# Layer kernel on one core: the second norm's scaling moved behind the feed-forward layers, a weight load issued later, and high-part passes ordered ahead of the low part

## The reference

```
h = layernorm(x, ln1_s, ln1_b)
q, k, v = h @ Wq + bq, h @ Wk + bk, h @ Wv + bv
x = x + (linear_attention(q, k, v) @ Wo + bo)
h = layernorm(x, ln2_s, ln2_b)
x = x + (relu(h @ W1 + b1) @ W2 + b2)
```

## Time and profile before

| what | us |
|---|---|
| median of 3 runs | 608.91 |
| lowest and highest of them | 607.68, 609.31 |
| the profiled execution, its own time | 609.01 |
| its span, first to last instruction | 607.1 |
| what lies around the span | 1.9 |

### The profile page before, as it was taken

One profiled execution on the slowest core, in us unless ns is written; L12 is line 12 of the kernel. 1 busy time (PEld: TensorE's weight loads), 2 busy tenths in 40 slices (PEclk: granted clock), 3 DMA queues, 4 the chain that ended last, 5 costly groups with the idle time before them and its releaser, 6 DMA issues.

```text
span 607.1 us, 13106 instructions
## 1 busy us (share of the span) xinstructions
PE 574.8 (95%) x4578; PEld 539.1 (89%) x4578; DVE 438.4 (72%) x1412; ACT 394.8 (65%) x1392; POOL 269.3 (44%) x431
## 2 busy tenths in 40 slices
PE   4889999999899999999999999999999999999977
PEld 3577899998899999998999999997899999998977
DVE  5856577677885777777896777777987665667774
ACT  4667676886575666677585666677675666566641
POOL 5343466664403436654404345646324334446310
PEclk9999999999999999999999999999999999999999
DMA  8500240040000000000000000000000000000000
GB/s 250 172 4 1 80 161 1 23 153 1 20 1 18 2 2 1 2 2 1 2 17 21 0 2 2 2 1 1 1 18 19 2 2 2 1 2 1 2 18 17
DMA packets 10785, 15.58 MB, mean 26 GB/s; under 512 B 969, under 2 KB 8221, under 8 KB 10337
## 3 DMA queue, kind: packets, MB, share of 16 engines
q1 hardware_dynamic: 8368, 11.47, 6.0%
q0 software_dynamic: 720, 2.30, 1.4%
q10 hardware_dynamic: 1632, 0.98, 0.5%
HBM read 12.61 MB, written 2.14 MB: 24 GB/s over the span
## 4 chain that ended last, share of the span: by engine, by line
PE 86%; DVE 5%; POOL 2%; ACT 2%; issue 2%; DMA 1%; SPq 1%; DVEq 0%; POOLq 0%
PE psD L1558 20%; PE psB L1558 19%; PE psA L1558 19%; PE psC L1558 19%; PE psD L1626 1%; PE psB L1626 1%; PE psA L1626 1%; PE psC L1626 1%; DMA wm<-in_wmod 1%; PE psB L1677 1%; PE psC L1677 1%; PE psA L1677 1%; DVE guC L1227 1%; POOL rstdB L817 1%; DVE guD L1101 1%
## 5 line engine op out<-in xcount | busy, mean ns | idle before, releaser
L817 POOL TENSOR_TENSOR rstdD<-msD,neghalf 128x2 f32<-128x2 f32 x36 | 26.2, 727 | 64.1 <-ACT ziD L452 46.8
L817 POOL TENSOR_TENSOR rstdC<-msC,neghalf 128x2 f32<-128x2 f32 x36 | 25.1, 699 | 50.7 <-ACT eqkC L452 50.5
L817 POOL TENSOR_TENSOR rstdA<-msA,neghalf 128x2 f32<-128x2 f32 x36 | 25.6, 712 | 49.3 <-ACT eqkA L452 48.2
L817 POOL TENSOR_TENSOR rstdB<-msB,neghalf 128x2 f32<-128x2 f32 x36 | 25.8, 717 | 36.4 <-ACT eqkB L452 32.6
L452 ACT ACTIVATE eqkA<-xA 128x129 f32<-128x129 f32 x64 | 19.2, 303 | 24.2 <-DVE xA L1148 24.2
L1558 PE MATMUL psC<-w,H 128*128 128x128 f32 x256 | 31.3, 276 | 0.9 <-ACT H L475 0.9
L1558 PE MATMUL psB<-w,H 128*128 128x128 f32 x256 | 31.5, 276 | 0.0
L1558 PE MATMUL psD<-w,H 128*128 128x128 f32 x256 | 31.4, 276 | 0.0
L1558 PE MATMUL psA<-w,H 128*128 128x128 f32 x256 | 31.2, 275 | 0.0
L1558 PEld LDWEIGHTS psC<-w,H 128*128 128x128 f32 x256 | 29.9, 192 | 1.2 <-ACT H L475 1.2
L1558 PEld LDWEIGHTS psB<-w,H 128*128 128x128 f32 x256 | 29.8, 192 | 0.5 <-issue 0.5
(11 more groups left out here) (556 smaller groups left out, 2402.5 us busy)
## 6 DMA issues: line engine op xcount, KB each, us to landing
M<-modulation_rows SPq DMA_DIRECT2D x2, 1280.0 KB, 8.4
M<-modulation_rows SPq DMA_DIRECT2D x1, 2560.0 KB, 8.7
out<-X SPq DMA_DIRECT2D x16, 128.0 KB, 1.9
w<-in_attn_W POOLq DMA_DIRECT2D x1, 1024.0 KB, 8.5
M<-in_attn_W SPq DMA_DIRECT2D x3, 256.0 KB, 4.5
X<-in_attn_x_in ACTq DMA_DIRECT2D x2, 256.0 KB, 3.5
M<-in_attn_W ACTq DMA_DIRECT2D x1, 256.0 KB, 3.6
wo<-in_attn_Wo POOLq DMA_DIRECT2D x1, 256.0 KB, 3.6
```

What stands on the lines that cost most here:

```text
L817: pool.tensor_tensor(b.rstd[:, :], b.ms[:, :], neghalf[:, :], ALU.pow).then_inc(b.s_rstd.sem, 1)
```

## The change

**The second norm.** Since relu(s * y) = s * relu(y) for s > 0, the feed-forward layers can run on x without its scaling, if the bias is multiplied by the standard deviation instead and the result by its inverse. The change does that. `scale` is no longer called for even n. POOL's power now writes two numbers for each token and tile, standard deviation and inverse, from exponents 0.5 and -0.5, into two columns beside x. The transposes of the second norm read channels 1 to 127 of x and the column with the standard deviation, straight from x, and wait for POOL (channel 0 follows from the others, as the mean is zero; the folding matrix is changed for that). `add_bias` for the second bias waits for these transposes, since they now read what it overwrites. The `move` behind `contract` multiplies by the inverse and adds, in two operations of 128x128 instead of one of 128x256.

**High part first.** `expand` and `gate` run the passes with x_hi of both products of a call ahead of those with x_lo, and the wait for x_lo stands between them (before, it stood ahead of the first pass). The number of passes and weight loads is the same.

**The load of W2** goes from POOL's queue to SP's, behind the weights of layer 1.

**Order.** The written-out orders of all engines are changed in many places. Those that the prediction speaks of are shown.

```diff
             pool.dma_start(wo[:, :, :], Wo.rearrange("l k n -> k l n")).then_inc(s_wo, 16)
-            pool.dma_start(w2[:, :, :, :].rearrange("p l c n -> p (l c) n"),
-                           W2.rearrange("l (c p) n -> p (l c) n", p=P)).then_inc(s_w2in, 16)
...
                 sync.dma_start(w1[:, l, :], W1[l, :, :]).then_inc(s_w1[1], 16)
+                if l == 1:
+                    sync.dma_start(w2[:, :, :, :].rearrange("p l c n -> p (l c) n"),
+                                   W2.rearrange("l (c p) n -> p (l c) n", p=P)).then_inc(s_w2in, 16)
...
                     pool.wait_ge(b.s_squares.sem, b.s_squares.value(i, n))
+                    if n % 2 == 0:
+                        pool.tensor_tensor(b.xe[i % 2][:, :, X_STD:], b.ms[:, :].unsqueeze(2).to_broadcast([P, TILES, 2]),
+                                           halves[:, :, :], ALU.pow).then_inc(b.s_rstd.sem, 1)
+                        return
                     pool.tensor_tensor(b.rstd[:, :], b.ms[:, :], neghalf[:, :], ALU.pow).then_inc(b.s_rstd.sem, 1)
...
-                pool.wait_ge(b.s_normed.sem, b.s_normed.value(i, n))
+                if k == 0:
+                    pool.wait_ge(b.s_normed.sem, b.s_normed.value(i, l + 1))
+                else:
+                    pool.wait_ge(b.s_tps.sem, b.s_tps.value(i, n))
...
-                dve.tensor_tensor(x(b, i), b.ps[:, 0, 0:T].rearrange("p (t f) -> p t f", f=D), x(b, i), ALU.add)\
-                    .then_inc(b.s_moved.sem, 1)
+                if n % 2 == 1:
+                    dve.tensor_tensor(x(b, i), b.ps[:, 0, 0:T].rearrange("p (t f) -> p t f", f=D), x(b, i), ALU.add)\
+                        .then_inc(b.s_moved.sem, 1)
+                    return
+                for t in range(TILES):
+                    last = dve.scalar_tensor_tensor(x(b, i)[:, t, :], b.ps[:, 0, t * P:(t + 1) * P],
+                                                    b.xe[i % 2][:, t, X_RSTD:X_RSTD + 1], x(b, i)[:, t, :],
+                                                    ALU.mult, ALU.add)
+                last.then_inc(b.s_moved.sem, 1)
...
-                norm, src = (n + 1, b.xn) if n < 2 * LAYERS else (LAST, b.z)
-                pe.wait_ge(b.s_normed.sem, b.s_normed.value(i, norm))
+                if n % 2 == 1:
+                    src = b.xe[i % 2][:, :, 2:2 + D]
+                    pe.wait_ge(b.s_rstd.sem, b.s_rstd.value(i, n + 1))
+                else:
+                    src = b.xn if n < 2 * LAYERS else b.z
+                    pe.wait_ge(b.s_normed.sem, b.s_normed.value(i, n // 2 + 1))
...
+            def high_then_low(b, parts, low):
+
+                for n, (o, w_hi, w_lo) in enumerate(parts):
+                    mm(o, w_hi, b.x_hi[:, :], start=n == 0, stop=False)
+                    mm(o, w_lo, b.x_hi[:, :], start=False, stop=False)
+                if low is not None:
+                    pe.wait_ge(b.s_x_lo.sem, low)
+                for o, w_hi, w_lo in parts:
+                    last = mm(o, w_hi, b.x_lo[:, :], start=False, stop=o is parts[-1][0])
+                return last
+
             def expand(b, i, l, k):
 
-                pe.wait_ge(b.s_x_lo.sem, b.s_x_lo.value(i, 2 * l + 2))
-                if i == 0:
-                    pe.wait_ge(s_low, 2 * l + 2)
-                for c in (2 * k, 2 * k + 1):
-                    last = exact(b, b.ps[:, k, c % 2 * T:(c % 2 + 1) * T], w1_hi[:, l, c * P:(c + 1) * P],
-                                 w1_lo[:, l, c * P:(c + 1) * P])
-                last.then_inc(b.s_w1ps.sem, 1)
+                if k == 0:
+                    pe.wait_ge(b.s_xT.sem, b.s_xT.value(i, 2 * l + 2))
+                    if i == 0:
+                        pe.wait_ge(s_low, 2 * l + 2)
+                high_then_low(b, [(b.ps[:, k, c % 2 * T:(c % 2 + 1) * T], w1_hi[:, l, c * P:(c + 1) * P],
+                                   w1_lo[:, l, c * P:(c + 1) * P]) for c in (2 * k, 2 * k + 1)],
+                              b.s_x_lo.value(i, 2 * l + 2) if k == 0 else None).then_inc(b.s_w1ps.sem, 1)
```

Of the orders, ACT in step 0 (W2's means of layer 3 are taken out earlier), PE at the head of each step, and PE at the end of the layers:

```diff
                 query_exps(D_, i, 2)
+                if i == 0:
+                    less_w2_means(3)
                 squares(A, i, 7)
...
                 relu(C, i, 2, 0)
-                if i == 0:
-                    less_w2_means(3)
                 relu(C, i, 2, 1)
...
                 transposes(D_, i, 0)
+                transposes(A, i, 1)
                 transposes(B, i, 1)
                 transposes(C, i, 0)
-                transposes(A, i, 1)
...
                 transposes(C, i, 7)
+                expand(C, i, 3, 0)
                 logits(A, i)
-                expand(C, i, 3, 0)
                 expand(C, i, 3, 1)
                 transposes(D_, i, 7)
+                expand(D_, i, 3, 0)
+                expand(D_, i, 3, 1)
+                logits(B, i)
                 logits2(A, i)
                 gate(A, i, 0)
-                logits(B, i)
-                expand(D_, i, 3, 0)
-                expand(D_, i, 3, 1)
                 logits2(B, i)
```

and DVE and PE at the start (chains A and B of step 0):

```diff
 # DVE
+            modulation(1)
+            low_part(A, 0, 0)
...
-            low_part(A, 0, 0)
-            modulation(1)
...
 # PE
-            transposes(B, 0, 0)
             project_queries(A, 0, 0)
             sums(A, 0, 0)
+            transposes(B, 0, 0)
+            attend(A, 0, 0)
             project_keys(B, 0, 0)
             project_queries(B, 0, 0)
-            attend(A, 0, 0)
             out_project(A, 0, 0)
             sums(B, 0, 0)
+            attend(B, 0, 0)
             out_project2(A, 0, 0)
-            attend(B, 0, 0)
             fold_weights(2)
             out_project(B, 0, 0)
             out_project2(B, 0, 0)
-            fold_weights(3)
             for i in range(STEPS):
+                if i == 0:
+                    fold_weights(3)
                 transposes(D_, i, 0)
```

More of the change, by code:

```diff
@@ L171, in program @@
             n = "ABCD"[c]
-            b.xe = [sb(f"x{n}{k}", [P, TILES, D + 1]) for k in range(2)]
+            b.xe = [sb(f"x{n}{k}", [P, TILES, XW]) for k in range(2)]
             b.stat = sb("stat" + n, [P, TILES, 6])
@@ L451, in squares @@
                 for t in range(TILES):
-                    last = act.activation(unused[:, t, :], b.xe[i % 2][:, t, :], ACT.Square, scale=float(D) ** -0.5,
+                    last = act.activation(unused[:, t, :], b.xe[i % 2][:, t, 0:1 + D], ACT.Square, scale=float(D) ** -0.5,
                                           accum_out=b.ms[:, t:t + 1])
@@ L568, in _ @@
                 transposed(B, i, 2)
+                squares(D_, i, 2)
+                if i == 0:
+                    high(5)
+                relu(C, i, 0, 1)
                 transposed(D_, i, 1)
-                relu(C, i, 0, 1)
                 key_exps(B, i, 1)
@@ L1301, in _ @@
                 low_part(C, i, 0)
+                low_part(B, i, 1)
                 low_part(A, i, 1)
@@ L1316, in _ @@
                 scale(A, i, 3)
-                scale(C, i, 2)
                 move(B, i, 2)
                 low_part(A, i, 2)
-                move(D_, i, 1)
                 low_part(C, i, 1)
@@ L1323, in _ @@
                 positive_keys(A, i, 1)
+                move(D_, i, 1)
+                positive_queries(A, i, 1)
+                masked(A, i, 1)
+                low_part(B, i, 2)
                 if i == 0:
                     low(5)
-                scale(D_, i, 2)
-                positive_queries(A, i, 1)
-                low_part(B, i, 2)
-                masked(A, i, 1)
                 if i + 1 < STEPS:
@@ L1413, in _ @@
                     in_scale(C, i + 1)
+                move(C, i, 5)
                 scale(A, i, 7)
-                move(C, i, 5)
                 divided(D_, i, 2)
+                move(B, i, 6)
+                low_part(A, i, 6)
                 if i + 1 < STEPS:
                     in_scale(D_, i + 1)
-                scale(C, i, 6)
-                move(B, i, 6)
-                low_part(A, i, 6)
                 move(D_, i, 5)
@@ L1474, in _ @@
                 stats(B, i)
-                scale(D_, i, 8)
+                low_part(D_, i, 7)
                 low_part(A, i, 8)
-                low_part(D_, i, 7)
                 scale_last(B, i)
@@ L1496, in _ @@
                 leave(C, i)
+                gate_up(A, i, 2)
+                low_part(D_, i, 8)
                 stats(C, i)
-                gate_up(A, i, 2)
-                scale_last(C, i)
                 finish(B, i, 0)
@@ L1503, in _ @@
                 finish(B, i, 1)
-                low_part(D_, i, 8)
+                scale_last(C, i)
                 finish(A, i, 0)
```

383 lines of the change are left out of this document (186 added, 197 removed).

## The result

The changed kernel takes 613.27 us (median of 5; 613.05 to 615.56), the kernel before 608.55 in the same comparison: a ratio of 1.0083, 95% interval 1.0064 to 1.0102. It is slower by 0.8%, and lies above the range that the prediction gave. The profiled execution is the one of 613.27 us, with a span of 611.4.

The account below looks back on a forecast made before the run. PE's list was taken as the bound, so only its idle time could be won: start -0.8, step 0 -0.7, places -1.6, experts' stretch -0.8, together -3.9 from 609.0, gave 605.1 us (taken as 603 to 607); range 601.0 to 611.0.

Parts of the forecast that it names:

- the start: Ahead of the steps, PE's wait for `wm` shrinks once W2 leaves POOL's queue: -0.8 us, bounds -1.8 and +0.5.
- step 0: PE's 0.94 us wait for H near 116 goes, as layer 3's W2 means run earlier: -0.7 us, between -0.9 and 0.
- places: PE's waits for D's `scale`, C's x_lo and C's first transposes go, evictions partly replace them: -1.6 us, bounds -4.4 and +4.6.
- the experts' stretch: DVE's queue gets 0.86 us shorter a step, so the router's transposes wait less: -0.8 us, between 0 and -3.1.
- the first layers of C and D: Sign in the profile after: these layers would come up to 2 us earlier.
- PE's idle time in a step: Sign of failure: the prediction is wrong if this grows.
- POOL's power, +0.25: Second norm's power with 4 results instead of 2 takes 0.25 us more, between nothing more and doubling to 1.23.
- the rival: POOL's power is paid by the element, deciding from 1.2 us on; gains of places and experts go: 608.7 us, chance 0.10.
- High part first at nothing: Apart from the x_lo wait counted in places, the new order of passes costs nothing; at most 0.42 us gained a call.
- The move pair: DVE's `move` behind `contract` as two operations takes 0.62 us, +0.20 a move, hidden by PE's work for other chains.
- The slower one, at 612.1: `expand` right behind its own transposes idles PE 0.41 us for C, 0.41 + 1.13 for D each step; chance 0.15.
- Gaps only change place: Waits in layers and experts only move, so only start and step 0 gain, 1.5 us: 607.5 us, chance 0.15.

Follow-up runs that it names:

- run 13: W2's load put back on POOL's queue, against the kernel of 8: 607.27 us, ratio 0.9980 to the kernel before.
- run 1: The changed kernel with all orders ahead of the loop over steps as in the kernel before: 609.91 us, ratio 1.0033.
- run 10: The changed kernel with 20 matmuls of no use put into TensorE's waits in the start: 611.34 us, ratio 1.0043.
- run 3: The changed kernel with the last part of each step, from C's transposes for layer 3's second norm on, in the old orders: 612.26 us, ratio 1.0071.
- run 5: All changed functions and W2's load on SP, with the orders of the kernel before on all four engines: 610.37 us, ratio 1.0016.
- run 7: The changed kernel with the old start and the old orders for the end of each step, behind A's and B's down projections: 608.38 us, ratio 0.9987.
- run 6: The kernel before with only the passes changed, high part ahead of the wait for the low part: 610.46 us, ratio 1.0027.
- 8: Run 7's kernel with B's coefficients ahead of A's and B's `low_part` ahead of A's `in_enter` again: 606.21 us, ratio 0.9948; measured again 606.51, 0.9962.
- run 2: The kernel before with only W2's load moved to SP, behind layer 1's weights: 607.67 us, ratio 0.9986.
- 9: Run 7's kernel with one place of 8 put back at a time: coefficients 607.89 us, ratio 0.9978; `low_part` ahead of `in_enter` 607.66, 0.9985.
- 11: The kernel of 8 with POOL's power of the second norm at 6 results instead of 4: 616.24 us, ratio 1.0121 to the kernel before.
- 12: The kernel of 8 with POOL's power of the second norm at 2 results instead of 4 in the last two steps: 605.25 us, ratio 0.9948.

## Why the prediction was wrong

By its own terms, for the profiled executions: the start was to give 0.8 us and cost 3.2; step 0 was to give 0.7 and gave 0.75; places and the experts' stretch together were to give 2.4 and the steps lost 3.6 (1.44, 1.13 and 1.0 in the last); and 1.7 came back at the end through a fall of the clock that the kernel before happened to have there. Most of the single signs that it named came true; the first layers of C and D came later, not earlier, and PE's idle time in a step grew, which was its own sign of being wrong.

**The start, -0.8, is the step that failed most.** Its mechanism is there: `wm` lands in 2.9 us instead of the 6.9 of the earlier trace rows,

```profile
wm<-in_wmod SPq DMA_DIRECT2D x1, 256.0 KB, 2.9
```

PE's wait of 1.78 us for it is gone, and the matmul that stood behind it begins at 13.27 instead of 14.63:

```profile
13.27 1.03 PE L1562 MATMUL psC<-wm,condT 128*16 128x512 f32 x2
```

Among the old orders of the start the move of W2 is worth some 0.4 us (run 13). But the sum took every duration of the start from a profile that stood at 2.4 GHz from 15 us on, and had no term for the granted clock. That A and B go more one after the other it counted as a small loss of waiting. The new start cost 3.2 us, 2.6 of them by the clock (runs 1 and 10). The Trainium skill, "TensorE: Matmul & The Clock Gate", section "Terms", prices such a stretch at half its length; for 13.6 us that would be 6.8, an estimate. The start shows 2.6 to 3.2; PE has other limits there too (in the window from 20 us on it is busy for 3.92 of 5.00). In the layers, where matmuls follow each other without such gaps, the runs come close to the page's price: 1.6 us for a fall of 3.4 in run 3, and 1.6 for one of 3.4 in run 5.

**Places, -1.6, failed above all at the loop's end, which it didn't look at.** The three waits went as it said, and the 0.41 us of `expand` behind its own transposes came for C and D alike, 3.8 us for 8 x 0.41 = 3.3. What it missed are places the diff moves without naming them: the end of a step (0.6 us a step by run 7, where the timeline points at A's move), `in_enter` ahead of `low_part` (0.4) and, in the experts' stretch, the coefficients of A ahead of B's while `spread` still takes B first (0.2). That is 1.2 us a step, and the changed kernel lost 1.1 to 1.4.

**The experts' stretch, -0.8.** The wait it spoke of fell by 2.0, more than a quarter of 3.1, and the stretch is no shorter: 35.40 and 35.75 us against 35.15 and 35.72. The window that answers to the second of the earlier trace rows shows PE busy for less than before:

```profile
180.00:280.00 100.00, 98.99 (x826) 96.02 (x825) 68.58 (x214) 66.75 (x256) 53.22 (x73) 1.00 0.01 4
280.00:320.00 40.00, 37.07 (x297) 34.70 (x297) 33.65 (x128) 27.30 (x75) 15.43 (x24) 1.00 0.03 8
```

while the first shows PE busier in the layers, which took longer. Busy time of fixed windows compares badly when the work inside them has shifted by 3 us.

**POOL's power, +0.25, was sized right and placed wrong.** It rose by 0.31, within its bounds:

```profile
L826 POOL TENSOR_TENSOR xD<-msD,halves 128x4 f32<-128x4 f32 x16 | 16.4, 1026 | 13.5 <-ACT eqkD L457 13.5
...
L829 POOL TENSOR_TENSOR rstdA<-msA,neghalf 128x2 f32<-128x2 f32 x20 | 14.4, 718 | 56.5 <-ACT eqkA L457 52.0 <-ACT ziA L457 4.4
```

But it lies closer to the path than "no wait of note" allowed: 0.4 us a step in good orders, more at the loop's head, and 0.31 further the kernel is 9.7 us slower. The threshold of 1.2 us that the rival named lies between 1.02 and 1.34, where the runs put it too. The Trainium skill's rule ("GPSIMD Engine Reference", section 3.1) says that a cost goes by the element; 0.71, 1.02 and 1.34 us for 2, 4 and 6 results agree with it in kind, on top of a start of some 0.4 us (an estimate from these three), so four results aren't the double of two. In size they don't: a result of the power costs some 0.155 us, a column of the additions of the earlier trace rows 2.1 ns.

**Step 0, -0.7, held in its sum:** 0.75. The wait for H went as said; but only 0.40 of the 0.75 lie in the layers, where it stood, and 0.35 in the experts' stretch, so that the number fits so well is in part luck. **High part first at nothing** held, more strictly than said: alone it moves a wait and gains none (run 6). **The move pair** rose as forecast, two operations of 0.35 us, 0.61 for the pair; no run tested whether DVE hides it.

**The rivals.** The slower one, at 612.1, came nearest to the measured time, but by luck: it named `expand` behind its own transposes and 1.54 us of idle time for D in each step. D's wait there was 0.47, close to the 0.41 that the forecast had for it, and run 3, which put these places back, gained nothing between the ends of the steps. "Gaps only change place" was the truest of them for the layers and experts (runs 3, 5, 6 and the full steps of 8), but it let the start gain 0.8.

**Open.** Why the clock falls in one start and not in another with the same matmuls: run 2 shows it falling in some executions of one kernel and not in others, and no run here settles what decides it. One lead is in the traces. At the start of the program the matmuls are slow (one of 256 columns takes 0.63 us, later 0.38). Among the profiles with the same start (runs 1, 7, 8, 9, 11, 12) they became fast at 11.2 to 11.7 us in the three where the clock fell at 18, and at 12.2 to 14.4 in the five where it didn't. Across different starts this doesn't hold: in the kernel before it was 11.2, without a fall. Nor was it tried which single call of the new start brings it, and the second norm's new scaling was never run alone.

## What to carry to other kernels

Read the granted clock of the start before costing a change there: a start that is better on paper can lose more by the clock than the wait was worth, and matmuls of no use in TensorE's waits won most of it back here. When a diff reorders hand-written lists, go through every reordered call with the question of who waits for what it was moved behind, also those the change doesn't speak of; here the functions were worth nothing alone, and three unnamed places lost 1.2 us a step. With them and the start put back, the kernel was 0.4 to 0.5% faster than before, but by its start and step 0, not by its full steps. And compare stretches between the same instructions, not waits or busy time of fixed windows: the waits named here grew by 0.5 us a step where the step itself grew by more than 1.

## What the runs showed of the hardware

- TensorE's granted clock fell from 2.4 to 1.2 GHz within a window in which the profile has PE busy for 5.00 of 5.00 us (15 to 20 of the changed kernel); run 1 kept the full clock with the same busy share there.
- A fall of 3.4 us cost 1.6 us in layers that matmuls bound (runs 3 and 5); 13.6 us at the lower level in the start cost 2.6 (run 10).
- The same kernel, one execution after the other, took 605.21 us at a mean clock of 1.000 and 608.80 at 0.990 (run 2).
- POOL's power costs 0.71, 1.02 and 1.34 us for 2, 4 and 6 results for each partition, so about 0.155 us a result, where its addition of 2 columns took 0.194 us in all.
- The second part of `wm`, 256 KB, landed in 6.9 us behind W2's 1 MB on POOL's queue and in 2.9 without it; with W2 put back on POOL it took 6.5 (run 13).
